# A graph and mixture-of-experts kernel: second routing made tile by tile, second experts in one pipeline with gathers of kept rows and scatters into the output

## What is computed

```python
x = x + _L0_gnn_ref(_layernorm(x), ...)      # attention over edges, 8 heads
x = x + _L0_ffn_ref(_layernorm(x), ...)      # 8 experts, best 2 of each row
x = x + _L1_gnn_ref(_layernorm(x), ...)      # graph convolution, layer norm, gelu
x = x + _L1_ffn_ref(_layernorm(x), ...)      # 6 experts, best 1 of each row
```

```python
probs = softmax(x @ w_gating)                # 6 values a row
gate1 = max(probs); gate2 = second largest
gate1 = gate1 / (gate1 + gate2 + EPS)
xn = (x - mu) * rsqrt(var + LN_EPS) * gamma
hidden = gelu(xn @ w1[e])                    # 512 -> 256, e = argmax
out = gate1 * (hidden @ w2[e])               # 256 -> 512
```

## Time and profile before

| | |
|---|---|
| median of three runs | 993.29 us (992.58 to 995.33) |
| the profiled execution's own time | 998.04 us |
| its span | 996.3 us |
| mean granted TensorE clock | 0.925 of full |
| PE busy | 850.6 us (85%) |
| DVE, ACT, POOL busy | 579.3, 370.5, 196.3 us |
| moved by DMA | 126.17 MB |

### The profile page before, as it was taken

One profiled execution on the slowest core, in us unless ns is written; L12 is line 12 of the kernel. 1 busy time (PEld: TensorE's weight loads), 2 busy tenths in 40 slices (PEclk: granted clock), 3 DMA queues, 4 the chain that ended last, 5 costly groups with the idle time before them and its releaser, 6 DMA issues.

```text
span 996.3 us, 15762 instructions
## 1 busy us (share of the span) xinstructions
PE 850.6 (85%) x5046; PEld 571.9 (57%) x5047; DVE 579.3 (58%) x1825; ACT 370.5 (37%) x673; POOL 196.3 (20%) x380
## 2 busy tenths in 40 slices
PE   5989989999999999999992899998399998408980
PEld 2455555457777777777771677775144565406640
DVE  7488889168788877777652355555343268710113
ACT  1243443356566666666640333432000212204430
POOL 5000000000112210122114122121563144340004
PEclk9999999999999999999995899999599999558995
DMA  8649999972121161101057354521334402043317
GB/s 243 247 126 229 271 265 271 197 183 76 53 73 26 44 208 34 47 22 47 6 177 251 103 181 158 169 101 64 85 87 128 137 21 107 0 103 127 126 64 206
DMA packets 89631, 126.17 MB, mean 127 GB/s; under 512 B 39688, under 2 KB 49064, under 8 KB 89294
## 3 DMA queue, kind: packets, MB, share of 16 engines
q1 hardware_dynamic: 76110, 109.71, 37.3%
q0 software_dynamic: 13440, 15.43, 5.9%
HBM read 64.31 MB, written 60.75 MB: 126 GB/s over the span
## 4 chain that ended last, share of the span: by engine, by line
PE 73%; DVE 9%; issue 5%; POOL 5%; DMA 4%; ACT 3%; DVEq 0%; SPq 0%; POOLq 0%; ACTq 0%
PE ps L737 12%; PE ps L610 9%; PE ps L639 9%; PE ps L801 9%; PE ps L621 7%; PE ps L483 6%; PE ps L727 6%; PE ps L488 3%; PE ps L744 2%; PE ps L440 2%; PE ps L826 2%; DVE R_B L1356 2%; PE ps L721 1%; DVE R_A L1454 1%; POOL slots_d L1228 1%
## 5 line engine op out<-in xcount | busy, mean ns | idle before, releaser
L737 PE MATMUL ps<-R_B,R_A 128*128 x432 | 128.6, 441 | 1.3 <-ACT R_A L1021 0.8
L973 ACT ACTIVATE R_A<-R_A,neg_max 125x1250 f32<-125x1250 f32 x80 | 106.6, 1333 | 56.5 <-DVE neg_max L1454 56.4
L1454 DVE CUSTOM_DVE_ANT_0 R_A<-ps,R_B,neg_max 125x417 f32<-125x417 f32 (+1 forms) x160 | 97.6, 649 | 27.9 <-PE ps L610 27.9
L610 PE MATMUL ps<-R_B 64*125 64x417 f32 (+1 forms) x480 | 106.5, 544 | 1.5 <-ACT XN L918 1.5
L639 PEld LDWEIGHTS ps<-R_W,XN 125*64 125x64 f32 x1600 | 85.3, 136 | 23.9 <-issue 23.8
L621 PE MATMUL ps<-ident,R_A 125*125 125x125 f32 x800 | 98.6, 278 | 0.0
L621 PEld LDWEIGHTS ps<-ident,R_A 125*125 125x125 f32 x800 | 94.9, 188 | 1.5 <-DVE R_W L1461 0.7
L639 PE MATMUL ps<-R_W,XN 125*64 125x125 f32 x1600 | 94.7, 272 | 0.8 <-DVE counted L1508 0.8
L737 PEld LDWEIGHTS ps<-R_B,R_A 128*128 128x128 f32 x432 | 79.7, 195 | 22.6 <-issue 14.9
L980 ACT ACTIVATE R_W<-ps 125x500 f32<-125x500 f32 x120 | 66.1, 585 | 51.0 <-PE ps L621 51.0
L1139 POOL TENSOR_SCALAR rstd<-mv 125x1 f32<-125x1 f32 x50 | 16.5, 330 | 340.4 <-DVE mv L1270 301.2
(11 more groups left out here) (251 smaller groups left out, 1236.0 us busy)
## 6 DMA issues: line engine op xcount, KB each, us to landing
slots_d<-R_B SPq DMA_DIRECT2D x9, 2304.0 KB, 11.2
R_B<-in_L_ffn_w_dram SPq DMA_DIRECT2D x28, 512.0 KB, 6.6
R_A<-slots_d SPq DMA_DIRECT2D x42, 256.0 KB, 2.7
slots_d<-R_A SPq DMA_DIRECT2D x27, 256.0 KB, 2.1
counts_d<-R_A SPq DMA_DIRECT2D x10, 546.9 KB
logs_d<-R_B SPq DMA_DIRECT2D x10, 546.9 KB
R_B<-logs_d SPq DMA_DIRECT2D x10, 546.9 KB
R_B<-counts_d SPq DMA_DIRECT2D x10, 546.9 KB
```

What stands on the lines that cost most here:

```text
L610: pe.matmul(bank(2 * h + g % 2, P, z - a), QT[r:r + DH, j, i * P:i * P + P], KT[r:r + DH, j, a:z], start=True, stop=True).then_inc(S("s_ma ...
L737: ins = pe.matmul(bank(b, TM, width), lhs[:, c * TM:c * TM + TM], flat[:, bass.ds(e * (n * width) + c * width, width)], start=c == 0, stop ...
L973: act.activation(SC[u % 2][h], SC[u % 2][h], ACT.Exp, bias=neg_max[:, 2 * (u % 2) + h:2 * (u % 2) + h + 1], scale=-1.0, accum_out=den[:, 2 ...
L1454: dve.tensor_tensor_reduce(SC[u % 2][h][:, a:z], bank(2 * h + g % 2, P, z - a), LNB[i % 2][:, a:z], -1.0, least if t else 3.0e38, ALU.add, ...
```

## The change

It has six parts.

1. The routing of the last layer is made tile by tile inside the node loop. PE routes tile i into its own small result (`route_unit`), DVE picks its expert (`pick_one`) and finds its slots (`take_slots`), PE ranks (`rank_unit`) with the running counts carried from tile to tile. Each expert has its own fixed region of `CAP` = 1280 rows, so a row's place is known as soon as its tile is ranked. The tables of the tiles' experts and first rows are made after the tenth tile (`take_counts`, the function that the first experts use, now with parameters).
2. ACT makes the normed rows (`unit_rows`, now on ACT) in place of DVE; POOL makes one more small value for that (`shift`).
3. POOL scatters a tile's scaled rows inside the loop or right behind it (`scatter_unit`); the rows go into `slots0_d`, used a second time. `slots1_d`, its zeroing and `made1_d` are gone.
4. The rows of `slots0_d` are now 516 floats (2064 bytes). The four more floats hold the row's number in the graph (`token`), or 1,000,000 for "no row". They are written by the zero fill, the first scatter and the second scatter.
5. X goes to DRAM (`x_d`, 516 floats a row) tile by tile in the loop, and the gate later into the four last floats.
6. The second experts are one pipeline of 15 tiles written out, without a hardware loop. For each tile DVE reads its 128 row numbers (`take_tokens`), POOL gathers the kept rows of X with their gates (`gather_kept`), DVE makes gate x product + kept row in one instruction (`add_kept`), and POOL scatters 128 rows into the output (`scatter_made`). Rows with the number 1,000,000 are out of bounds and are left out by the DMA.

```diff
-MOVED_AT = {4: (0,), 5: (1,), 6: (2, 3), 7: (4, 5), 8: (6,), 9: (7, 8)}
+WIDE, NOWHERE = 516, 1000000
+RANKED_EARLY, PICKED_EARLY = {8: 2, 9: 4}, {8: 3, 9: 5}
+RANKED_LATE, PICKED_LATE = {6: 0, 7: 1, 8: 3, 9: 5}, {5: 0, 6: 1, 7: 2, 8: 4, 9: 6}
+SCATTERED_AT = {7: (0,), 8: (1,), 9: (2, 3)}
...
-    slots0_d = nc.dram_tensor("slots0_d", (ZEROED * TM, D), F32).ap()
-    slots1_d = nc.dram_tensor("slots1_d", (MT1 * TM, D), F32).ap()
-    made1_d = nc.dram_tensor("made1_d", (MT1 * TM, D), F32).ap()
+    slots0_d = nc.dram_tensor("slots0_d", (ZEROED * TM, WIDE), F32).ap()
+    x_d = nc.dram_tensor("x_d", (N, WIDE), F32).ap()
...
-            zero_tiles(slots1_d, 0, MT1)
...
-                sp.dma_start(rowsA[t % 3], slots0_d[bass.ds(base[t], TM), :]).then_inc(xs_in[t % 3], 16)
+                sp.dma_start(rowsA[t % 3], slots0_d[bass.ds(base[t], TM), 0:D]).then_inc(xs_in[t % 3], 16)
...
+            for i in range(T):
+                sp.wait_ge(S("ln_stat"), 3 * T + i + 1)
+                move(x_d[P * i:P * i + P, 0:D], X[:, i, :], S("x_kept"))
+
+            def load_rows1(t):
+
+                above_zero(sp, S("z_turned"), t - 2)
+                above_zero(sp, S("token_made"), t - 2)
+                first = sp.value_load(base_i[0:1, t:t + 1], min_val=0, max_val=(ZEROED - 1) * TM)
+                sp.dma_start(rows1[t % 3], slots0_d[bass.ds(first, TM), :]).then_inc(xs_in[t % 3], 16)
+            sp.wait_ge(S("slot1_made"), 1)
             sp.wait_ge(S("rows1_out"), 16 * T)
-            mix_loads(slots1_d, made1_d, MT1 // LANES, xs_in, S("z_turned"), y_out, S("yy_moved"))
-            for i in range(T):
-                sp.wait_ge(S("x_stored"), i + 1)
-                move(out[P * i:P * i + P, :], X[:, i, :], S("out_done"))
-            sp.wait_ge(S("out_done"), 32 * T)
-            sp.wait_ge(S("zeros_out"), 16 * (T + 1))
+            for t in range(3):
+                load_rows1(t)
+            sp.wait_ge(S("gate1_made"), 1)
+            move(x_d.rearrange("(i p) w -> p i w", p=P)[:, :, D:WIDE], gate_rows, S("x_kept"))
+            for t in range(3, MT1):
+                load_rows1(t)
+            for k in range(3):
+                sp.wait_ge(rows_out[k], SCATTERED0[k] + 16 * len(range(k, MT1, 3)))
...
+            def route_unit(i):
+
+                pe.wait_ge(S("xt_moved"), 2 * T + i + 1)
+                above_zero(pe, S("log1_taken"), i)
+                for c in range(C):
+                    ins = pe.matmul(bank(2, P, E1), XT[:, c, i * P:i * P + P], gate_w[:, c, 0:E1],
+                                    start=c == 0, stop=c == C - 1)
+                ins.then_inc(S("log1_made"), 1)
+
+            def rank_unit(i):
+
+                pe.wait_ge(S("mask1_made"), i + 1)
+                pe.matmul(bank(3, 126, 8), before[0:126, 0:126], counted[:, i % 2, :], start=True, stop=True)\
+                  .then_inc(S("rank1_made"), 1)
+            for k in range(5):
+                project(5 + k)
+                if k == 0:
+                    pe.wait_ge(S("agt_moved"), 3 * C)
+                turn_unit(k)
+                if k > 0:
+                    route_unit(k - 1)
+                if k > 1:
+                    rank_unit(k - 2)
+            for k in range(5, 8):
+                turn_unit(k)
+                route_unit(k - 1)
+                rank_unit(k - 2)
+            route_unit(7)
+            rank_unit(6)
+            turn_unit(8)
+            route_unit(8)
+            rank_unit(7)
+            turn_unit(9)
+            route_unit(9)
+            rank_unit(8)
+            rank_unit(9)
+
+            pe.wait_ge(S("slot1_ready"), T)
+            pe.matmul(bank(6, 1, 8), ident[0:126, 125:126], counted[:, T % 2, :], start=True, stop=True)\
+              .then_inc(S("count_made"), 1)
...
+            turn_rows1(0)
+            for t in range(MT1 + 1):
+                if t >= 1:
+                    turn_hidden(t - 1)
+                if t < MT1:
+                    hidden_product(t)
+                if t + 1 < MT1:
+                    turn_rows1(t + 1)
+                if t >= 1:
+                    output_product(t - 1)
...
+            def unit_rows(i):
+
+                act.wait_ge(S("ln_rstd"), 3 * T + i + 1)
+                act.activation(XM[i], X[:, i, :], ACT.Identity, bias=shift[0:P, i:i + 1], scale=rstd[0:P, i:i + 1])\
+                   .then_inc(S("xn_made"), 1)
...
+            pool.iota(zero_rows[:, D:WIDE].bitcast(I32), [[0, WIDE - D]], base=NOWHERE, channel_multiplier=0)\
+                .then_inc(S("zero_made"), 1)
...
+                pool.wait_ge(S("ln_stat"), 3 * T + j + 1)
+                link(pool.tensor_scalar(r, mv[0:P, j, 1:2], 1.0, LN_EPS, ALU.mult, ALU.add))
+                link(pool.tensor_tensor(r, r, half_pow[0:P, 0:1], ALU.pow))
+                pool.tensor_scalar(shift[0:P, j:j + 1], mv[0:P, j, 0:1], r, -1.0, ALU.mult, ALU.mult)\
+                    .then_inc(S("ln_rstd"), 1)
...
+            def scatter_unit(i):
+
+                pool.wait_ge(S("slot1_ready"), i + 1)
+                pool.wait_ge(S("xg_made"), i + 1)
+                pool.indirect_dma_start(slots0_d, bass.IndirectOffsetOnAxis(ap=slot[:, 0, i:i + 1], axis=0),
+                                        scaled[i], None).then_inc(S("rows1_out"), 16)
+            scattered = 0
             for j in range(T):
                 rstd_tile(S("hg_stat"), j + 1, j, None, S("hg_rstd"))
                 if j:
                     next_norms(j - 1)
+                if j == T - 4:
+                    pool.wait_ge(S("agg_made"), 3 * C)
+                    for i in range(T):
+                        ins = pool.iota(scaled[i][:, D:WIDE].bitcast(I32), [[0, WIDE - D]], base=P * i,
+                                        channel_multiplier=1)
+                    link(ins)
+                    for i in range(T):
+                        pool.wait_ge(rows_in[i], 16 * K0)
+                for i in SCATTERED_AT.get(j, ()):
+                    scatter_unit(i)
+                    scattered = i + 1
             next_norms(T - 1)
...
+            for i in range(scattered, T):
+                scatter_unit(i)
+
+            def gather_kept(t):
+
+                pool.wait_ge(S("token_made"), t + 1)
+                above_zero(pool, S("yy_moved"), t - 2)
+                pool.indirect_dma_start(kept1[t % 3], None, x_d,
+                                        bass.IndirectOffsetOnAxis(ap=token[:, t:t + 1], axis=0),
+                                        bounds_check=N - 1, oob_is_err=False).then_inc(rows_in[t % 3], 16)
+
+            def scatter_made(t):
+
+                pool.wait_ge(S("yy_moved"), t + 1)
+                pool.indirect_dma_start(out, bass.IndirectOffsetOnAxis(ap=token[:, t:t + 1], axis=0),
+                                        made1[t % 3], None, bounds_check=N - 1, oob_is_err=False)\
+                    .then_inc(rows_out[t % 3], 16)
+            pool.wait_ge(S("x_kept"), 32 * (T + 1))
+            for t in range(MT1 + 2):
+                if t < MT1:
+                    gather_kept(t)
+                if t >= 2:
+                    scatter_made(t - 2)
...
+            def pick_one(i):
+
+                dve.wait_ge(S("log1_made"), i + 1)
+                dve.tensor_copy(logits[:, i, 0:E1], bank(2, P, E1)).then_inc(S("log1_taken"), 1)
+                dve.wait_ge(S("log1_taken"), i + 1)
+                link(dve.max(top[:, i, :], logits[:, i, :]))
+                link(dve.max_index(top_i[:, i, :], top[:, i, :], logits[:, i, :]))
+                link(dve.tensor_copy(pick[:, i, 0:1], top_i[:, i, 0:1]))
+                dve.tensor_scalar(counted[0:P, i % 2, :], iota8[:, :], pick[:, i, 0:1], None, ALU.is_equal)\
+                   .then_inc(S("mask1_made"), 1)
+
+            def take_slots(i):
+
+                dve.wait_ge(S("rank1_made"), i + 1)
+                dve.wait_ge(S("mask1_made"), i + 1)
+                link(dve.tensor_copy(counted[:, (i + 1) % 2, :], bank(3, 126, 8)))
+                link(dve.tensor_tensor_reduce(work[:, 0, :], counted[0:P, i % 2, :], counted[0:P, (i + 1) % 2, :],
+                                              1.0, 0.0, ALU.mult, ALU.add, slot_f[:, 0, i:i + 1]))
+                dve.tensor_copy(slot[:, 0, i:i + 1], slot_f[:, 0, i:i + 1]).then_inc(S("slot1_ready"), 1)
+
+            dve.wait_ge(S("counts_reset"), 1)
+            link(dve.memset(logits[:, :, :], -3.0e38))
+            for j in range(T):
+                add_bias(j)
+                if j in PICKED_EARLY:
+                    take_slots(RANKED_EARLY[j])
+                    pick_one(PICKED_EARLY[j])
+                scale_shift(j)
+                if j:
                     add_layer(j - 1)
+                if j > 2:
+                    scaled_rows(j - 3)
+                if j in RANKED_LATE:
+                    take_slots(RANKED_LATE[j])
+                if j in PICKED_LATE:
+                    pick_one(PICKED_LATE[j])
+            add_layer(T - 1)
+            scaled_rows(T - 3)
```

(18 more changed lines are left out.)

407 lines of the change are left out of this document (143 added, 264 removed).

## The result

The changed kernel took 966.39 us (median of four runs, 962.75 to 971.97) against 992.93 us (four runs) of the kernel before beside it: ratio 0.974, 95% interval 0.968 to 0.980. In a second comparison it took 965.51 us (five runs, 964.54 to 966.29) against 995.56 us (nine runs): ratio 0.969 [0.967, 0.971]. The forecast was 960 us in a range of 950 to 974. The profiled execution has a span of 966.1 us where the kernel before had 996.3; forecast was 963.1.

The account below looks back on a forecast made before the run. Before: a DVE-POOL node loop, a serial piece without PE, PE-bound experts, a tail without PE. Span 996.3 - 13.4 - (29.4 - 6.9) + (68.6 - 67.9) + 2 = 963.1; the 33.2 us gain from the median gives 960 us, range 950 to 974.

Parts of the forecast that it names:

- S: Start of the last tile's scaling in the node loop, 851.49 us before the change, forecast at 857.2.
- Node loop: Periods from tile 5 to 9 sum to 31.5 us against 25.7, so the last tile's scaling starts 5.7 us later.
- S to experts: From the last tile's scaling to PE's first expert transposition: 28.4 us against 47.5, with POOL's scatter queue late next.
- Experts: Second experts, PE full: fifteen tiles at 4.33 us, plus half clock, filling and draining, 68.6 us in all.
- Tail: From the last add to the end: one add and one scatter to landing, 6.9 us against 29.4.
- Start: Zero fill with wider rows, 2064 bytes for 2048, in a full DMA: 2 us longer, bounds 0 and 8.
- wide rows at the start: Rival: zero rows at shifted addresses move slower and attention starts late, 8 us in place of 2, 966 us; chance 0.15.
- the shorter chain: Rival: scatters land sooner, DVE's small rows hide beside POOL, the start costs nothing; 952 us; chance 0.12.
- The longer chain: Rival: in the node loop and routing, a late rank or pick holds DVE's next scaling; +11, 971 us; chance 0.15.
- POOL in the experts: Rival: two indirect DMAs a tile bound the second experts from 4.33 us a pair; at 7.0, about 1000 us; chance 0.08.

Follow-up runs that it names:

- the late scaling: Changed kernel with scaled rows put back to five tiles behind in DVE's order, not three: 962.66 us, ratio 0.966 to the kernel before.
- the early scatters: Changed kernel with POOL's scatters 1 and 3 ahead of the norms and 2 a round earlier: 963.79 us, ratio 0.968 to the kernel before.
- the version with both edits: Changed kernel with scaled rows five tiles behind and POOL's scatters 1 to 3 earlier: 957.80 us, ratio 0.962 to the kernel before.

## Why the prediction was right, and where it was off

The mechanism was right: S later, the experts nearer to S, the tail gone. By its own steps, in the profiled execution:

- **Node loop: S + 5.7 forecast, + 9.8 measured.** From tile 5 to tile 9 are 31.5 us (829.83 to 861.32), and 31.5 were forecast, but in part by luck. The single periods are 7.5, 7.6, 8.2 and 8.2 where 6.8, 8.1, 8.3 and 8.3 stood: DVE's own rows took longer than I had added up, and POOL's ten iotas, priced at 1.3, ran while it had nothing else to do. What failed is the sentence that up to tile 4 PE sets the pace as before. The change also shortens the lag of the scaled rows from five tiles to three. The first is written over counts that the aggregation still reads, so it waits for PE's last piece (818.96), and in DVE's order it stands ahead of `add_bias(4)`: 5.68 us, of which 4.1 reach tile 5. This is shown by the late scaling. I had priced the scaled row's duration and not its wait: a wait that costs nothing behind tile 5 does where it now stands.
- **S to experts: 28.4 forecast, 30.9 measured.** The last norms start at S + 9.3 (8.5 forecast), mostly since one of the scatters ahead of them took 1.77 us. The last scatter starts at S + 20.1 (19.2) and lands after 7.2 us (6.5 taken). Between landing and load stand 1.0 us in which SP reads a row number; I had left that out. That POOL's queue of scatters is late next was right: the early scatters show it for the two ahead of the last norms, and the last slots, ready 1.7 us before they are used, for the six behind them.
- **Experts: 68.6 forecast, 66.8 measured**, 67.9 before. A tile takes 4.10 us (907.64 to 911.74), not 4.33: 3.5 us less for fifteen. The 4.33 was read from rounds of three. Most of the difference is in the transpositions, 0.82 us of a tile before and 0.65 now, which stand in other groups; why they are shorter wasn't tried. Against this, filling, draining and seams come to 2.9 us (64.4 at the full clock, less 61.5) and not 1.2. The half clock costs 2.4 us in this execution (66.8 less 64.4), as forecast. PE has no wait for POOL or DVE in the experts, though POOL's first gather of kept rows starts only at 897.8: that it costs nothing was right.
- **Tail: 6.9 forecast, 7.1 measured**, and some 22 us between the medians with and without it (22.5 forecast). That the gathers, adds and stores go is the mechanism, and it is shown. That 6.9 was so near is luck: it was an add and a landing of 6.0 us. The last scatter carries no rows and lands after 2.1, at 962.7, and the rest is a closing instruction of POOL (DRAIN, L93) from 960.3 to 965.9, which I had at nothing. In the version with both edits it takes 5.5 us too, with two more gathers a tile 10.3; what it waits for wasn't tried.
- **Start: 2 us forecast, nothing measured.** The scaling of tile 3 stands at 811.18 before and 811.16 after. Bytes alone (0.7 us) would have been the better end of the bound.

The sum of the errors, 4.1 + 2.5 - 1.8 + 0.2 - 2.0 = 3.0, is the distance from 963.1 to 966.1. The median of 966.39 is 6.4 us above the forecast of 960. The other 3.4 come from the step from span to median: the profiled execution before was 4.75 us above its median, and I took the same for the changed kernel, whose profiled execution is only 1.4 above its own.

Of the rivals, wide rows at the start and the shorter chain are refuted as they were put. The longer chain came near in size (6.6 us of the 11) by chance and was wrong in its place: no scaling waited for a late rank or pick. Only DVE's own rows for slots and picks stand ahead of the last scaling, for some 0.3 us: POOL's root is through at 861.0, the scaling starts at 861.3. POOL in the experts is real and far off.

The executions with and without wide rows also bear on the rule of the Trainium skill (DMA: Bandwidth & Descriptors, How a descriptor splits into AXI transactions) by which I had estimated 4 to 6 us for the start. Nothing of that size shows, in a stage whose DMA share is 1.15. The section speaks of bytes that are fetched, and here the shifted side is the one that is written; whether shifted reads pay, no run here shows.

## What to carry to other kernels

When a change writes an engine's program in a new order, look up for every moved instruction not only how long it takes but what it waits for at its new place, and what is queued behind it. Add up a period from the work in it, and price the seams on their own, since a new order has other ones. Look at what ends the kernel even when the sum comes out right. A store that goes straight to its final place removes more than itself: here gathers, adds and stores of the whole output, some 22 of 28 us. Streaming the routing gave the other 6.5; two orders of instructions, one on DVE and one on POOL, held back as much again.
